# Two steps of a second attention's query, batch 1, moved from VectorE to GpSimd

## What is computed

```python
    def _L1_xattn_ref(q, k, v, Wq, bq, Wk, bk, Wv, bv, Wo, bo, ln_g, ln_b):
        qn = _layer_norm(q, ln_g, ln_b)
        qp = qn @ Wq.T + bq
        kp = k @ Wk.T + bk
        vp = v @ Wv.T + bv
        ...
        scores = jnp.einsum('bhqd,bhkd->bhqk', qh, kh) * scale
        attn = jax.nn.softmax(scores, axis=-1)
        out = jnp.einsum('bhqk,bhkd->bhqd', attn, vh)
        ...
        return out @ Wo.T + bo
    x = x + _L0_xattn_ref(_layernorm(x, axis=-1), ...)
    x = x + _L0_ffn_ref(_layernorm(x, axis=-1), ...)
    x = x + _L1_xattn_ref(_layernorm(x, axis=-1), ...)
    x = x + _L1_ffn_ref(_layernorm(x, axis=-1), ...)
```

## Time and profile before

| | us |
|---|---|
| three runs | 254.31, 252.95, 253.52 |
| median | 253.52 |
| the profiled execution | 252.5 |
| its span on the core | 250.7 |
| TensorE busy | 222.7 (89%) |
| VectorE busy | 185.8 (74%) |
| ScalarE busy | 156.1 (62%) |
| GpSimd busy | 79.5 (32%) |

### The profile page before, as it was taken

The page is one execution under the profiler, slowest core; times in us unless marked ns, Lnnn a source line. Parts: engine busy times, 40 slices in busy tenths (PEclk is TensorE's granted clock), DMA queues, the critical chain, the costliest instruction groups (busy, mean ns, idle before and its releaser), DMA issues.

```text
span 250.7 us, 5109 instructions
## 1 busy us (share of the span) xinstructions
PE 222.7 (89%) x1656; PEld 138.6 (55%) x1656; DVE 185.8 (74%) x578; ACT 156.1 (62%) x228; POOL 79.5 (32%) x228
## 2 busy tenths in 40 slices
PE   2879889999999999989897889999988989989970
PEld 1464445555555558976785444444534447768760
DVE  7779776777777476678558988888775657789974
ACT  6775897677875761521323567877767674796660
POOL 4581445465612100100201252444412042344321
PEclk9999999999999999999999999999999999999999
DMA  6779899921010048600050773300000000000000
GB/s 210 271 220 162 198 164 173 327 67 43 24 65 0 3 90 167 124 0 0 9 165 18 276 230 95 97 3 0 4 0 3 0 1 3 1 0 3 0 21 22
DMA packets 18180, 20.41 MB, mean 81 GB/s; under 512 B 1553, under 2 KB 15609, under 8 KB 17825
## 3 DMA queue, kind: packets, MB, share of 16 engines
q1 hardware_dynamic: 17578, 19.16, 29.7%
q10 hardware_dynamic: 576, 0.94, 1.2%
HBM read 15.90 MB, written 4.19 MB: 80 GB/s over the span
## 4 chain that ended last, share of the span: by engine, by line
PE 53%; DVE 18%; issue 11%; ACT 6%; POOL 5%; DMA 4%; SPq 1%; DVEq 0%; POOLq 0%; ACTq 0%
PE bank L384 10%; PE bank L459 9%; PE bank L437 8%; PE bank L433 5%; PE bank L577 3%; PE bank L557 3%; DVE row_max L885 3%; PE bank L558 3%; DVE st L1071 2%; ACT probs L1396 2%; POOL rs L1719 2%; PE bank L390 2%; PE bank L632 2%; ACT k_stack L1363 2%; DMA aw<-in_attn_w 2%
## 5 line engine op out<-in xcount | busy, mean ns | idle before, releaser
L1396 ACT ACTIVATE probs<-bank 128x1024 f32<-128x1024 f32 x64 | 64.4, 1023 | 16.2 <-PE bank L437 11.1
L882 DVE CUSTOM_DVE_ANT_0 discard<-bank,bias_q 128x512 bf16<-128x512 f32 x64 | 42.5, 689 | 15.8 <-PE bank L384 14.4
L384 PE MATMUL bank<-k_stack,q_stack 72*128 72x512 bf16 x128 | 47.3, 383 | 3.9 <-DVE row_max L885 1.8
L885 DVE TENSOR_REDUCE row_max<-bank 128x1 f32<-128x512 f32 x64 | 42.0, 687 | 9.2 <-PE bank L384 6.7
L437 PE MATMUL bank<-q_stack,k_stack 102*128 102x256 bf16 x256 | 43.7, 272 | 0.2 <-ACT q_stack L1381 0.2
L459 PE MATMUL bank<-probs,v_ext 128*32 128x256 f32 x512 | 37.4, 388 | 0.6 <-ACT probs L1396 0.2
L437 PEld LDWEIGHTS bank<-q_stack,k_stack 102*128 102x128 bf16 x256 | 24.8, 98 | 17.2 <-issue 1.4
L1381 ACT COPY q_stack<-bank 6x512 bf16<-6x512 bf16 x32 | 18.5, 577 | 21.5 <-PE bank L406 21.4
L1637 POOL CAST max_part<-row_max 128x4 bf16<-128x4 f32 x32 | 6.2, 194 | 76.0 <-DVE row_max L885 44.5
L384 PEld LDWEIGHTS bank<-k_stack,q_stack 72*128 72x128 bf16 x128 | 12.2, 96 | 23.4 <-DVE row_max L885 9.8
L433 PE MATMUL bank<-bias_k,idb 128*128 128x512 bf16 x64 | 24.3, 380 | 0.5 <-ACT probs L1396 0.3
(11 more groups left out here) (191 smaller groups left out, 362.9 us busy)
## 6 DMA issues: line engine op xcount, KB each, us to landing
k_stack<-k_bounce SPq DMA_DIRECT2D x9, 384.0 KB
q_bounce<-q_part SPq DMA_DIRECT2D x12, 192.0 KB, 2.6
k_bounce<-early SPq DMA_DIRECT2D x4, 384.0 KB, 2.8
experts_w<-in_wu SPq DMA_DIRECT2D x1, 1024.0 KB, 4.9
early<-in_wu SPq DMA_DIRECT2D x1, 1024.0 KB, 7.2
experts_w<-in_wg SPq DMA_DIRECT2D x1, 816.0 KB, 14.5
experts_w<-in_wu SPq DMA_DIRECT2D x1, 816.0 KB, 16.0
experts_w<-in_wd SPq DMA_DIRECT2D x1, 768.0 KB, 16.6
```

Source lines behind the costliest of these rows:

```text
L384: mm(bank[:, qt, :], q_stack[0:STACK, b, h, qt * 128:(qt + 1) * 128], k_stack[0:STACK, b, h, :], start=True, stop=True).then_inc(for_max, 1)
L882: ins = dve.tensor_tensor_reduce(discard[:, qt, :], bank[:, qt, :], bias_q[:, qt, :], 1.0, LOWEST, ALU.add, ALU.max, o)
L885: ins = dve.tensor_reduce(o, bank[:, qt, :], AX.X, ALU.max)
L1396: act.activation(probs[:, n % (2 * HG), :], bank[:, at:at + 2, :].rearrange("p a n -> p (a n)"), ACT.Exp, scale=SCALE).then_inc(exp_done, 1)
```

## The change

The normalisation of batch 1 and the third part of its query leave VectorE's list. GpSimd's list gets them: the normalisation behind the reciprocal root of batch 1, in group 18's place and ahead of the split of group 19; the third part behind the split of group 20, with a wait for ScalarE's second part (`q_second`) and for the remainder. The instructions are the same, their semaphores too. Batch 0's steps stay where they are.

```diff
@@ VectorE @@
             attention(1, [
                 (3, lambda: add_experts0(1)),
                 (5.5, lambda: stats0(1)),
-                (7, lambda: normalise("a1n", 1, res[2][1])),
                 (9.5, lambda: q_remainder(1)),
-                (10.5, lambda: q_third(1)),
                 (27.5, lambda: attT_copy(1, 0)),
@@ GpSimd @@
+            def last_normalise():
+
+                pool.wait_ge(rstd_ready["a1n"], B)
+                for t in range(QT):
+                    pool.tensor_scalar(norm["a1n"][1][:, t, :], res[2][1][:, t, :], mean_var["a1n", 1][:, t, 0:1],
+                                       rstd["a1n", 1][:, t:t + 1], ALU.subtract, ALU.mult).then_inc(normed["a1n"], 1)
+
+            def last_third():
+
+                pool.wait_ge(q_second, B)
+                pool.wait_ge(q_rest_ready, B)
+                pool.tensor_tensor(q_part[1][:, 2, :], q_rest[:, :], q_part[1][:, 1, :], ALU.subtract).then_inc(q_parts[B + 1], 1)
...
                 (18, lambda: root("a1n", 1)),
+                (18, lambda: last_normalise()),
+                (20, lambda: last_third()),
                 (19, lambda: add_row(2, 1, "bo1")),
```

## The result

The changed kernel is slower. Its median is 255.26 us (20 runs, 253.94 to 258.17) against 253.56 us for the kernel before (20 runs beside it, 252.89 to 257.12). The ratio is 1.0074, with a 95% interval of 1.0054 to 1.0094. That is 1.7 us by the medians and 1.9 by the ratio, where the prediction had -0.3. The profiled execution took 254.07 us, with a span of 252.3.

A forecast was written before the change was run, and what follows sets the result against it. VectorE was taken to lead into the entrance, TensorE from then on. Normalisation -0.29 and third part 0 gave -0.29 us: 252.2 from the profiled 252.5, 253.2 from the median 253.52; range 252.4 to 254.1.

The forecast's parts named there:

- The bound and the place: TensorE leads after the entrance; VectorE time saved there counts only where TensorE waits, in front of batch 1's transposes.
- The hole of 0.29: TensorE could begin batch 1's transposes at 146.71 but begins at 147.00; closing this whole gives -0.29 us.
- The price of the normalisation on GpSimd: Two moved instructions right behind the reciprocal root, 0.35 us each, ending at 146.47, before TensorE needs them.
- d: Time of one moved normalisation instruction on GpSimd: taken as 0.35 us, between a cast's 0.28 and add_row's 0.73.
- The formula behind it: GpSimd's second normalisation instruction ends at 145.77 + 2d; with about 0.05 for the semaphore, TensorE may start at 145.82 + 2d.
- The slower rival: GpSimd late with the normalisation before the transposes: +0.04 at d = 0.61, +0.28 at 0.73, +1.2 at 1.2; chance 0.18.
- The third part: Query's third part moved from VectorE to GpSimd, about 0.73 us there: term 0, bounded by -0.10 and +0.2.
- What is queued behind on GpSimd: Group 19's split of maxima and later GpSimd work still come before their readers: cost zero.
- A rule against the change: GpSimd's price against VectorE's for two inputs of 128x256: 0.73 against 0.41, 1.8 times.
- break-even of 0.59: Value of d at which TensorE's transposes would start at 147.00, as before the change.
- A neighbour's slowing: VectorE and GpSimd working side by side could slow each other; beside VectorE's reductions from PSUM nothing was charged.

The follow-up runs named there:

- split: Kernel before, with GpSimd normalising batch 1's first tile of tokens and VectorE the second, third part on VectorE: 252.63 us, ratio 0.9971.
- norm_only: Changed kernel with the third part of the query back on VectorE, only batch 1's normalisation on GpSimd: 254.69 us, ratio 1.0052.
- dve_late: Kernel before, plus an addition of 384 columns that nobody reads on VectorE ahead of its normalisation: 254.52 us, ratio 1.0039.
- filled: Changed kernel with three more filler products on TensorE ahead of the transposes: 253.79 us, ratio 1.0008.
- third_only: Changed kernel with the normalisation back on VectorE, only the third part of the query on GpSimd: 253.22 us, ratio 0.9997.
- costs: Kernel before, plus ten extra instructions of several forms on GpSimd where it is idle, from 101.5: one run, 253.79 us.
- fill_first: Changed kernel with its own three filler products moved ahead of the transposes, none added: 253.69 us, ratio 0.9989.
- split_holes: Kernel before with the normalisation split between GpSimd and VectorE, and three fillers moved into TensorE's waits ahead of the transposes: 252.04 us, ratio 0.9962.

## Why the prediction was wrong

- **The bound and the place: right.** The hole of 0.29 in front of the transposes was the only place where the change met TensorE, and what happened there reached the rest. Closed to 0.09 (split) it gave 0.20 in the stage, open to 0.80 it took 0.51.
- **The price of the normalisation on GpSimd: the step that failed.** "The operation has one wide input, like the cast ... so I take d = 0.35, nearer to the cast." It measured 0.80, over both ends of the range of 0.28 to 0.73. The number of wide inputs alone is not what sets the price on GpSimd: with two inputs the same width costs 0.40. The formula behind it held: 145.82 + 2 x 0.80 = 147.42 against 147.00 gives +0.42, and +0.51 was seen, since the first instruction started 0.11 behind the root (not 0.08) and the two, of 0.80 and 0.81, lasted 1.60 together, an overlap of 0.01 (not 0.06).
- **The price of a late hand-over: mis-sized too.** The slower rival priced it at its length, +0.28 for d = 0.73, and needed d = 1.2 for a loss over 0.5%. Its place, direction and break-even were right; the clock was missing. The counts give (15/20 - 18/97) x 1.48 = 0.8 us for it, with 0.5 for the wait. Together with the unexplained 0.13 that makes 1.5 of 1.7 to 1.9 us. This prices each low run at one fall, and that is too little for some: 7 of the changed kernel's 20 runs have a mean clock of 0.984 or less (median 256.95), against 8 of 97 before, while the two executions with one fall at this place stand at 0.987 and 0.989. Where those runs lost the rest no profile shows; more slow starts than in the kernel before could also be in the remainder. That the changed kernel's own low runs fell in this same place is inferred from norm_only, dve_late and filled; no profile of the changed kernel caught one.
- **The third part: right.** 0 as predicted (third_only 0.9997). GpSimd took 0.67 where 0.73 was forecast, waited 1.86 for ScalarE, and stood idle 0.75 more before group 21's maxima came.
- **What is queued behind on GpSimd: right.** Group 19's split ended about 149.36, 0.9 before TensorE asked for it at 150.23.
- **A rule against the change: it deserved more weight.** The rows had a price for it: GpSimd's 0.73 against VectorE's 0.41 with two inputs of 128x256, 1.8 times. That factor alone puts d at 0.61, past the break-even of 0.59. The factor measured for the moved instruction, with one wide input, is 0.80 to 0.34, 2.4.
- **A neighbour's slowing: right to charge nothing.** The form took 0.80 beside VectorE's reductions and 0.80 beside other work in costs; no run shows it with VectorE idle throughout. Not every neighbour is harmless: in dve_late a cast of 4 columns on GpSimd took 0.46 in place of 0.19 beside VectorE's addition (0.55 from 146.99).

## What to carry to other kernels

Price a moved instruction by a row of the same operation and form on the new engine, and where there is none take the range wide: neither the number of inputs nor the width alone set GpSimd's price (0.80 with one wide input, 0.40 with two, 0.58 at half the width). A wait in front of TensorE had two prices here, its length (0.51 us) and a fall of the clock in a part of the runs (1.48 us in norm_only); one profiled execution can miss the second, so read the mean clocks of all the runs. Where TensorE carries fillers to keep busy, put them into its waits rather than behind them: in filled and fill_first no run had a low clock, and in split_holes they took no time of their own.

## What was not expected of the hardware

- GpSimd's tensor_scalar of 128x128 took 0.65 to 0.81 with two operations (costs, changed) and 0.60 or 0.61 with one (costs), a two-input subtraction 0.40 (costs) and a cast 0.28.
- With 0.5 us more of waiting, more than half of the runs had a low mean clock (15 of 20, 7 of 12 and 7 of 12, against 18 of 97). Where a profile shows the fall (norm_only, dve_late), the granted clock goes from 1.00 to 0.50 and 0.51 of full speed, and the fall costs 1.48 and 1.45 us. With 0.65 us of filler in the same hole (filled, fill_first) it was 0 of 12 in each. In the 1.50 us from 0.13 before the score tile on, TensorE was busy 0.78 in dve_late, where the clock then fell, and 0.74 in the changed kernel and 1.37 in filled, where it stayed at 1.00. How idle TensorE has to be, and for how long, no run shows.
- The same six products near the start took 2.74 us in nine profiled executions and 4.36 (costs) to 5.13 (norm_only) in the other five, at a granted clock of 1.00 in both; between the kernel before and the changed one that moved all that follows by 0.9 us.
